# Late weight pieces split without GpSimd, and a routing slot table written by 48 indirect DMAs, in a fused token, attention and expert kernel

## What is computed

```python
h = _L0_tok_ref(x, ...)                      # state-space kernel: 8 x 256 tokens of 512
h = jnp.concatenate([h, txt], axis=1)        # + 128 text tokens: 8 x 384 = 3072 rows of 512
h = h + _L0_attn_ref(_layernorm(h), ...)     # latent attention, one head of 64
h = h + _L0_ffn_ref(_layernorm(h), ...)      # experts

def _L0_ffn_ref(...):
    scores = softmax(h @ gate_weight.T)                       # 8 experts in 4 groups
    topk_w, topk_i = _group_limited_topk(scores)              # 2 groups, then 2 experts
    g = einsum('th,nfh->ntf', h, gate_w); u = einsum('th,nfh->ntf', h, up_w)
    e = einsum('ntf,nhf->nth', silu(g) * u, down_w)           # F = 352
    routed = einsum('nth,tn->th', e, wmat)
    shared = silu(h @ sh_gate_w.T) * (h @ sh_up_w.T) @ sh_down_w.T   # width 704
    return routed + shared
```

## Time and profile before

| | |
|---|---|
| median of 3 runs | 969.4 us (968.99 to 970.17) |
| profiled execution | 966.46 us, span 964.6 us |
| mean granted clock | 0.967 |
| TensorE (PE) busy | 829.0 us, 86% |
| VectorE busy | 513.3 us, 53% |
| ScalarE busy | 395.0 us, 41% |
| GpSimd busy | 349.4 us, 36% |
| chain that ended last | PE 72%, DVE 12%, ACT 6%, POOL 3%, issue 3%, DMA 2% |

### The profile page before, as it was taken

The page is one execution under the profiler, slowest core; times in us unless marked ns, Lnnn a source line. Parts: engine busy times, 40 slices in busy tenths (PEclk is TensorE's granted clock), DMA queues, the critical chain, the costliest instruction groups (busy, mean ns, idle before and its releaser), DMA issues.

```text
span 964.6 us, 20136 instructions
## 1 busy us (share of the span) xinstructions
PE 829.0 (86%) x7301; PEld 522.5 (54%) x7302; DVE 513.3 (53%) x919; ACT 395.0 (41%) x683; POOL 349.4 (36%) x352
## 2 busy tenths in 40 slices
PE   0009999989799999699859997999999999999993
PEld 0009997655355545355436553666666666666661
DVE  7997746656652544736776442455434444444441
ACT  5863324334223232537442153454444444444441
POOL 0056744413810011524331032344444444444442
PEclk9999999989989999999979998999999999999996
DMA  5021234044412003597342054354444544444542
GB/s 191 0 66 47 59 111 143 24 88 121 111 45 66 1 24 108 135 225 160 92 90 80 23 153 155 79 89 83 83 79 85 87 87 76 79 85 86 87 76 33
DMA packets 66046, 84.68 MB, mean 88 GB/s; under 512 B 36096, under 2 KB 36224, under 8 KB 65344
## 3 DMA queue, kind: packets, MB, share of 16 engines
q0 software_dynamic: 12480, 29.37, 17.4%
q1 hardware_dynamic: 41408, 31.48, 11.8%
q10 hardware_dynamic: 12096, 22.94, 8.7%
HBM read 48.38 MB, written 27.53 MB: 79 GB/s over the span
## 4 chain that ended last, share of the span: by engine, by line
PE 72%; DVE 12%; ACT 6%; POOL 3%; issue 3%; DMA 2%; ACTq 0%; DVEq 0%; POOLq 0%
PE PS L2087 10%; PE PS L2089 10%; PE PS L2088 10%; PE PS L1075 7%; PE PS L590 6%; PE PS L1076 6%; PE PS L1077 6%; PE PS L2097 3%; PE PS L746 2%; PE PS L2119 2%; PE PS L1276 2%; PE PS L1233 1%; PE PS L2028 1%; DVE work L1422 1%; PE PS L1234 1%
## 5 line engine op out<-in xcount | busy, mean ns | idle before, releaser
L2087 PE MATMUL PS<-big,work 128*128 x605 | 200.9, 332 | 4.1 <-ACT work L2165 2.4
L2089 PE MATMUL PS<-big,work 128*128 x605 | 201.2, 333 | 0.0
L2088 PE MATMUL PS<-big,work 128*128 x605 | 201.2, 332 | 0.0
L2274 POOL DMA_INDIRECT out_dram<-work x55 | 88.0, 1600 | 62.5 <-DVE work L2244 46.0
L2206 DVE SCALAR_TENSOR_TENSOR work<-work,PS 128x352 f32<-128x352 f32 x55 | 28.7, 522 | 154.0 <-PE PS L2089 154.0
L2165 ACT ACTIVATE work<-PS 128x1024 f16<-128x1024 f16 x55 | 56.3, 1024 | 85.2 <-PE PS L2097 85.2
L2087 PEld LDWEIGHTS PS<-big,work 128*128 128x128 f16 x605 | 59.3, 98 | 42.6 <-issue 6.7
L2089 PEld LDWEIGHTS PS<-big,work 128*128 128x128 f16 x605 | 59.4, 98 | 42.2 <-issue 0.3
L2088 PEld LDWEIGHTS PS<-big,work 128*128 128x128 f16 x605 | 59.2, 98 | 36.5 <-issue 0.3
L994 POOL TENSOR_TENSOR big<-work,big 128x544 f16<-128x544 f32 (+1 forms) x30 | 38.0, 1267 | 108.8 <-ACT work L980 108.8
L2261 POOL DMA_INDIRECT big<-x_dram,work x55 | 55.8, 1015 | 46.7 <-POOL work L2258 45.0
(11 more groups left out here) (284 smaller groups left out, 1754.2 us busy)
## 6 DMA issues: line engine op xcount, KB each, us to landing
work<-in_weights ACTq DMA_DIRECT2D x36, 272.0 KB, 2.8
work<-in_shared ACTq DMA_DIRECT2D x28, 256.0 KB, 3.3
x_dram<-big SPq DMA_DIRECT2D x24, 256.0 KB, 2.3
out_dram<-big SPq DMA_DIRECT2D x24, 256.0 KB, 3.5
big<-in_weights ACTq DMA_DIRECT2D x20, 272.0 KB, 2.9
big<-in_weights SPq DMA_DIRECT2D x1, 2176.0 KB, 9.8
big<-in_par SPq DMA_DIRECT2D x1, 1185.0 KB, 10.7
big<-in_c_real SPq DMA_DIRECT2D x1, 1024.0 KB, 5.8
```

Of the source, the lines that this page charges most:

```text
L2087: pe.matmul(out, x_high, w_high, start=start, stop=False)
L2088: pe.matmul(out, x_high, w_low, start=False, stop=False)
L2089: return pe.matmul(out, x_low, w_high, start=False, stop=stop)
L2274: pool.indirect_dma_start(out_d, bass.IndirectOffsetOnAxis(ap=S_NUM[u][:, 0:1], axis=0), YO[u], None, compute_op=ALU.add).then_inc(s_add, 16)
```

## The change

- Low halves: all of them are made by VectorE with `split_low`; `ON_POOL`, the scaled copies on ScalarE (L980) and `split_low_g` go. Low halves of shared pieces 11 to 16 get places in VectorE's list between units 4 and 11.
- Late pieces are staged in five places, in turn 2, 3, 1, 0, 6; place 6 is the room of two row tiles that are stored by then. Places 2 and 3 move to the end of the first block, since the masks no longer need its start. The first five loads are issued at once behind ScalarE's unit 45, further ones up to three splits ahead, where the place was freed two splits earlier. The second half of block 0 uses places 0, 1, 6; the last block keeps 4, 5, 0, 1. The late splits skip some units (91 to 98 have four, 99 none) and end with unit 107 instead of 111; block 0 no longer waits for the table.
- Norm rows 18 to 23 alternate with units 50 to 55 on VectorE and ScalarE.
- Slot table: the eight mask turns go. VectorE computes for each (choice, row) the address of its slot in a DRAM table, and a payload of token number and weight. GpSimd issues 48 indirect writes of 128 entries of 8 bytes, waits for all of them and loads the table (128 x 440 bytes) back. A DMA fills the DRAM table with padding entries early in the kernel. The address list is ready behind unit 81. `route_experts` is in two parts with two units between, `count` stands in front of unit 80, and the table of weight offsets (`route_offsets`) is made behind unit 82.
- GpSimd: `bias` of pair 1 moves behind the first three low rows, those of pairs 2 and 3 behind `c_scale` of pairs 2 and 3 and unit 14. The first three gathers stand behind the table load, the low halves of block 0, and the stores of the normalised rows.
- TensorE starts the routed stage when the offsets and all low halves are there; its first turning waits for the gather.

```diff
-        STAGE_LATE = STAGE + [cut(big, 6 * D + k * PIECE, PIECE) for k in range(2)] + [cut(work, ro_at + k * PIECE, PIECE) for k in range(2)]
-        assert 3 * AW * P + 2 * PIECE <= 3 * D + GCH * S + S and 6 * D + 2 * PIECE <= BLK and 2 * PIECE <= 3 * D
+        STAGE_LATE = STAGE + [cut(big, BLK - (2 - k) * PIECE, PIECE) for k in range(2)] + [cut(work, ro_at + k * PIECE, PIECE) for k in range(2)]
+        STAGE_LATE.append(cut(big, HT0 + slot_of(0, 2) * D, PIECE))
+        assert 3 * AW * P + 2 * PIECE <= 3 * D + GCH * S + S and 6 * D + 2 * PIECE <= BLK and PIECES == 8 and 2 * PIECE <= 3 * D
...
+            pool.dma_start(slots_d.rearrange("(p t) c -> p (t c)", p=P), a["pad"]).then_inc(s_slots0, 16)
...
-            k = q - FIRST_OF[0]
-            return q % 4 if k < 0 else k % 2 if k < 4 else (4, 5, 0, 1)[k % 4]
-
-        ON_POOL = tuple(range(MCH, SHARED_PIECES)) + tuple(
-            q for q in range(SHARED_PIECES, SPLITS) if (q - SHARED_PIECES) % 2 or 16 <= q - SHARED_PIECES < 40)
+            k = q - SHARED_PIECES
+            whole, last = (len(LATE_BLOCKS) - 2) * PIECES + PIECES // 2, (len(LATE_BLOCKS) - 1) * PIECES
+            return (2, 3, 1, 0, 6)[k % 5] if k < whole else (0, 1, 6)[k % 3] if k < last else (4, 5, 0, 1)[k % 4]
...
+            eng.wait_ge(sp_low, q + 1)
...
+        AHEAD = tuple(range(5, SHARED_PIECES)) + tuple(range(SHARED_PIECES + 5, SPLITS))
+
         def ahead(q):
-            return next(k for k in (1, 2, 3) if k == 3 or PLACES[q] in PLACES[q - k - 1:q])
+            last = max((k for k in range(q) if PLACES[k] == PLACES[q]), default=q - 5)
+            return max(1, min(3, q - last - (1 if q < SHARED_PIECES else 2)))
...
+            if PLACES[q] in (4, 5):
+                eng.wait_ge(ff_p, 6 * SH_UNITS + MCH)
+            if PLACES[q] == 6:
+                for b in range(2):
+                    eng.wait_ge(s_out[b], 3 * 16)
...
-                act.wait_ge(ro_v.sem, ro_v.at("slot_tok"))
...
-            if q in ON_POOL:
-                act.wait_ge(sp_high, q + 1)
-                act.activation(stage(q), stage(q), ACT.Copy, scale=W_SCALE).then_inc(sp_scaled, 1)
...
-            ffn_tensor(pe, 64, 74)
+            ffn_tensor(pe, 64, 80)
             count(pe)
-            ffn_tensor(pe, 74, 80)
-            for q in range(TABLE_TURNS):
-                make_table(pe, q)
-                ffn_tensor(pe, 80 + 2 * q, 82 + 2 * q)
-            ffn_tensor(pe, 96, B * SH_UNITS)
+            ffn_tensor(pe, 80, B * SH_UNITS)
...
-            ffn_split_vector(dve, 46, 47, q)
-            for w in range(3):
-                out_stats(dve, 3, w)
+            ffn_vector(dve, 46, 47)
+            out_stats(dve, 3, 0)
+            out_stats(dve, 3, 1)
+            ffn_split_vector(dve, 47, 48, q + 1)
+            out_stats(dve, 3, 2)
             moments(dve, 3, "a")
-            ffn_split_vector(dve, 47, 49, q + 1)
-            for w in range(3, 6):
-                out_stats(dve, 3, w)
+            ffn_split_vector(dve, 48, 49, q + 2)
+            out_stats(dve, 3, 3)
+            out_stats(dve, 3, 4)
+            ffn_split_vector(dve, 49, 50, q + 3)
+            out_stats(dve, 3, 5)
             moments(dve, 3, "b")
-            norm_rows(dve, 18)
-            ffn_split_vector(dve, 49, 51, q + 3)
-            norm_rows(dve, 21)
-            ffn_split_vector(dve, 51, 56, q + 5)
+            norm_row(dve, 18)
+            ffn_split_vector(dve, 50, 51, q + 4)
+            for k in range(5):
+                norm_row(dve, 19 + k)
+                ffn_split_vector(dve, 51 + k, 52 + k, q + 5 + k)
...
-            route_experts()
+            route_experts_1()
             ffn_split_vector(dve, 72, 74, q + 26)
+            route_experts_2()
+            ffn_split_vector(dve, 74, 78, q + 28)
             route_counts()
-            ffn_split_vector(dve, 74, 76, q + 28)
+            ffn_split_vector(dve, 78, 80, q + 32)
             route_slots()
-            ffn_split_vector(dve, 76, 78, q + 30)
+            ffn_split_vector(dve, 80, 82, q + 34)
             route_table()
-            ffn_split_vector(dve, 78, 80, q + 32)
-            for u in range(3):
-                dve.wait_ge(s_x2[u], B * 16)
-            route_masks(0)
-            for k in range(TABLE_TURNS):
-                if k + 1 < TABLE_TURNS:
-                    route_masks(k + 1)
-                route_add(k)
-                if k < 3:
-                    ffn_split_vector(dve, 80 + 2 * k, 82 + 2 * k, q + 34 + 2 * k)
-                else:
-                    ffn_vector(dve, 80 + 2 * k, 82 + 2 * k)
-            ffn_split_vector(dve, 96, 104, q + 40)
-            ffn_split_vector(dve, 104, 112, q + 48)
+            ffn_split_vector(dve, 82, 83, q + 36)
+            route_offsets()
+            ffn_split_vector(dve, 83, 91, q + 37)
+            for k in range(4):
+                ffn_vector(dve, 91 + 2 * k, 93 + 2 * k)
+                split_low(dve, q + 44 + k)
+            ffn_vector(dve, 99, 100)
+            ffn_split_vector(dve, 100, 108, q + 49)
+            ffn_vector(dve, 108, B * SH_UNITS)
...
-            bias(pool, 1)
             c_scale(pool, 1, 1, 2)
             for i in range(PAIRS - 1):
                 for half in range(2):
                     deviation(pool, i, "ab"[half])
                     rows_low(pool, 6 * i + 3 * half)
-                    if i == 0 and half == 1:
-                        for q in range(MCH, SHARED_PIECES):
-                            split_low_g(pool, q)
+                    if i == 0 and half == 0:
+                        bias(pool, 1)
+                    if i == 1 and half == 1:
+                        c_scale(pool, 2, 2, PAIRS)
+                        pool.wait_ge(ff_p, SH_UNITS + 1)
                         bias(pool, 2)
-                    if i == 1 and half == 1:
                         bias(pool, 3)
-                        c_scale(pool, 2, 2, PAIRS)
-            late = iter(ON_POOL[SHARED_PIECES - MCH:-6])
-            deviation(pool, 3, "a")
-            split_low_g(pool, next(late))
-            deviation(pool, 3, "b")
-            split_low_g(pool, next(late))
-            rows_low(pool, 18)
-            split_low_g(pool, next(late))
-            rows_low(pool, 21)
-            for q in late:
-                split_low_g(pool, q)
+            for half in range(2):
+                deviation(pool, 3, "ab"[half])
+                rows_low(pool, 18 + 3 * half)
+            slot_writes(pool, 0, 2 * NT)
+            pool.wait_ge(s_scat, 16 * 2 * NT)
+            pool.dma_start(SLOTS.rearrange("p t c -> p (t c)").bitcast(U32), slots_d.rearrange("(p t) c -> p (t c)", p=P)).then_inc(
+                s_slots, 16)
+
+        def slot_writes(pool, n0, n1):
+            for n in range(n0, n1):
+                if n == 0:
+                    pool.wait_ge(s_slots0, 16)
+                    pool.wait_ge(ro_v.sem, ro_v.at("w1"))
+                k, t = divmod(n, NT)
+                pool.indirect_dma_start(slots_d, bass.IndirectOffsetOnAxis(ap=IDX[:, k, t:t + 1], axis=0),
+                                        PAY[:, n, :].bitcast(U32), None).then_inc(s_scat, 16)
...
+            for k in range(5):
+                load_piece(act, q + k)
+            ffn_splits(act, 46, 51, q)
+            for k in range(5):
+                row_high(act, 18 + k)
+                ffn_splits(act, 51 + k, 52 + k, q + 5 + k)
+            row_high(act, 23)
+            ffn_splits(act, 56, 64, q + 10)
...
-            ffn_splits(act, 64, 86, q + 18)
-            ffn_scalar(act, 86, 96)
-            ffn_splits(act, 96, 112, q + 40)
+            ffn_splits(act, 64, 90, q + 18)
+            for k in range(4):
+                ffn_scalar(act, 90 + 2 * k, 92 + 2 * k)
+                splits(act, q + 44 + k, q + 45 + k)
+            ffn_scalar(act, 98, 99)
+            ffn_splits(act, 99, 107, q + 48)
+            ffn_scalar(act, 107, B * SH_UNITS)
...
-            nc.vector.scalar_tensor_tensor(SL, SLT, -float(P), SL, ALU.mult, ALU.add).then_inc(did("row"), 1)
+            nc.vector.tensor_scalar(SL, SL, float(SLOT_TILES), None, ALU.mult).then_inc(did("i56"), 1)
+            own()
+            nc.vector.scalar_tensor_tensor(IDX, SLT, 1.0 - P * SLOT_TILES, SL, ALU.mult, ALU.add).then_inc(did("idx"), 1)
             for k in range(2):
+                nc.vector.tensor_copy(PAY[:, k * NT:(k + 1) * NT, 0].bitcast(U32), lc("token")).then_inc(did(f"tok{k}"), 1)
+            for k, m in enumerate((M0, M1)):
                 own()
-                nc.vector.tensor_tensor(TOKV[:, k, :], lc("token"), SL[:, k, :], ALU.subtract).then_inc(did(f"tok{k}"), 1)
+                nc.vector.tensor_copy(PAY[:, k * NT:(k + 1) * NT, 1], m).then_inc(did(f"w{k}"), 1)
...
-            late = iter(ON_POOL[-6:])
-            for q in late:
-                if q == ON_POOL[-4]:
-                    pool.wait_ge(ro_v.sem, ro_v.at("slot_tok"))
-                    pool.wait_ge(s_pad, 1)
-                    for b in range(2):
```

(55 more changed lines are left out.)

88 lines of the change are left out of this document (24 added, 64 removed).

## The result

The changed kernel takes 976.3 us (median of 15 runs, 970.4 to 979.1), the kernel before 970.4 us beside it. The ratio is 1.005, with a 95% interval from 1.003 to 1.007: slower by half a per cent, where I had said 925 us. The profiled execution of after took 978.4 us, with a span of 976.1. Of the run with earlier entries, further down, one of four executions (952.8 us) fell in a slower state of the core and is left out of its time.

The account below looks back on a forecast made before the run. TensorE was busy in most slices, so only less waiting, work or throttling would help. Savings of 23 + 6 + 6 + 4 + 1.5 + 7 less 3 gave 44.5 us: 966.46 to 922, 925 as median; 80% range 914 to 952.

Parts of the forecast that it names:

- part 1: Slot table: 96 table matmuls and the mask waits leave TensorE, 23 us saved; 48 indirect writes on GpSimd come in.
- c: Cost of each indirect write on GpSimd: 1.05 us, taken from the gather; bounds 0.97 below, 1.60 or 1.85 above.
- my own formula: First gathered tile ready at 489.3 + 47c us, 539 for c = 1.05, ahead of the shared units' end at 550.
- Waits removed: TensorE's late shared-FFN waits: first mask 9.9, selection 4.5, low halves at 409 and 583 us, 1.5 before the first turning.
- a thin cover: VectorE's added splits in units 64 to 81 just use up the available time; 3 us of new waiting charged.
- Parts 2 and 3 together: Low halves on VectorE (6, 4 and 1.5 us saved, 3 charged) and the new order on GpSimd (7 us saved).
- Part 3: Order on GpSimd: biases of pairs 2 and 3 behind the last scale remove waits between 200 and 300 us; 7 us.
- "Nothing" for the bias of pair 1: Moving it behind the first three low rows, where GpSimd idles, was to change nothing.
- the count: Moved from before unit 74 to before unit 80; selection wait and half of that stretch's clock loss go: 6 us.
- B: Rival: cover too thin, VectorE sets the pace in units 64 to 81, 10 us more, 941 or a little less; 18%.
- A: Rival: the writes bind at 1.6 to 1.85 us each, so the routed stage waits for the gather; 939 to 951; 25%.
- C: Rival: VectorE's two-input splits hold up every write, 2.6 us each, table ready at 611; slower, 985 us; 5%.

Follow-up runs that it names:

- the run with earlier entries: Changed kernel with copies ahead of all writes but the first 8 and last 10, and indices and entries worked out before units 80 and 81: 934.9 us, ratio 0.968.
- the fastest kernel: Changed kernel with entries worked out ahead of units 80 and 81, a copy ahead of each of the first 38 writes, the last 10 bare: 927.9 us, ratio 0.956.
- the run with 24 landed writes: Changed kernel with only the 24 first-choice writes, each waiting until the one before has landed; half of the entries left out: 921.7 us.
- the run with copies: Changed kernel with a small GpSimd copy, waited for, ahead of each of the 48 indirect writes: 945.3 us.

## Why the prediction was wrong

The step that failed is in part 1: the writes were taken as a cost on GpSimd's queue alone, with the question when the table is ready. What they do to the other engines was no term of the sum. The earlier trace rows gave me a duration, from gathers and scatters that never follow each other closely; in the earlier trace rows the gather starts 2.1 us after the last one, and no two indirect DMAs of before are closer. I used it for 48 in a row, a pace that the trace of before does not contain, and kept both ends for the duration but none for the effect on others. What the runs show in its place: 48 writes 1.30 us apart hold up the other engines and cost the kernel 48 us. This is nearly the whole of the miss of 51 us: 976.3 less 48 is 928, and the run with the first 38 writes paced, the last ten bare and the entries worked out earlier has 927.9. Pacing alone gave 945.3, since it makes the table late.

Point by point:

- **c.** 1.05 forecast, 0.96 + 0.30 = 1.27 measured, inside the bounds. By my own formula the table is then ready at 549 us, just in time for 550. What follows the last write was shorter than taken: in the fastest kernel 1.4 us to land and 2.2 for the load (issued at 547.4, its reader at 549.6), not 3.6 and 4.0.
- **Start of the writes.** 477 forecast; 479.4 to 487.5 in runs with the order of after, 473.6 and 474.7 with the early entries. The changed kernel's profiled run was late by some 6 us before any write: unit 69's addition is at 450.9 there, at 444.3 in the run with 24 landed writes.
- **Waits removed.** As forecast, the mask, the selection and the low halves at 409 and 583 us are gone, and in the run with 24 landed writes the 1.5 before the first turning (0.3 there). The 3 us charged for a thin cover were some 5: 4.3 us for low halves, now at 402 and 480 us, and 1.1 for a product at 474, where before had none of those.
- **Parts 2 and 3 together.** 6 + 4 + 1.5 + 7 - 3 = 15.5 forecast. Measured 21 us by the medians (18 to 26 by the interval), 15.5 by the two spans.
- **Part 3.** 7 forecast, 7.3 measured. "Nothing" for the bias of pair 1 looks too little: with the new order the first product of the shared FFN is at 215.8 us, before at 213.5. If that is its doing, the rest gained more than I took.
- **The sum.** 925 forecast for a case without a hole; without one, 921.7 us (one execution, half of the entries) and 927.9. Some of this agreement is luck: parts 2 and 3 brought more than forecast, so part 1 with the count brought less.
- **Rivals.** B came in small: one wait of 2.8 us for a low half ahead of 480.6 us, where I had 10 us. A came once the hole was gone (17.2 us in the run with copies), not in after. C had the right sign from the wrong mechanism: it let VectorE slow the writes, and no write of after took over 1.43 us. From 519 to 546 us, with VectorE idle in after, all 22 writes took 0.96 us; in the run with a copy at each, with VectorE at work, 7 of 18 there took 1.03 to 1.37 and the rest 0.96, and all 7 lay beside a VectorE operation with two SBUF inputs. The Trainium skill (SBUF — State Buffer, Who interferes with whom) has such contention; these rows agree in sign, with 0.4 us more at most; the 3.1 us a write of that page's other section did not come. The harm that counted went the other way, from GpSimd to the others. 5% for slower was too little for an operation whose pace no trace had shown.
- **What would show it.** The listed sign "writes start at 470 to 485, 1.0 to 1.3 us apart" came true but for 1 us (485.9) while the time was wrong; the sign that failed was that no wait over 3 us would stand in this stretch.

## What to carry to other kernels

A duration taken from isolated instances prices the instruction, not a row of them: ask whether the trace has ever seen that pace, and if not, give "everyone else slows down" a place among the rivals with a size of its own. When several engines fall idle at once and the profile names no releaser, look at what the one busy engine is doing, and change its pace first; here a useless 0.2 us copy ahead of each indirect DMA won 31 us (976.3 to 945.3), and earlier entries with bare last writes another 17. Read a hole by its kind: late starts with idle DMA engines and late landings with busy ones look alike in the slices and need opposite remedies.

## What was unexpected of the hardware

- Indirect DMAs of GpSimd 1.22 to 1.30 us apart on average hold up instruction starts on TensorE, VectorE and ScalarE from about the 12th on, in after for up to 20.0 us at a time (ScalarE's silu), and down to one TensorE instruction each 1.40 us. At 1.41 to 1.46 us some of it is left, from 1.52 us on nothing is seen. Writes and reads do it alike, 128 or 64 rows alike; 48 plain DMAs 0.53 us apart do not.
- An indirect DMA of 64 rows takes 0.90 us and one of 128 rows 0.96: nearly all of it is fixed.
- One profiled run a kernel is a weak measure of a few us: by the two spans the order on GpSimd gained 2.0 us (964.6 to 962.6), by the medians 7.3.
